# Two bias rows of a vision tower: from TensorE and ScalarE to adds on GpSimd

## The reference, cut to what matters

```
def _L0_ffn_ref(x, W1, b1, W2, b2):              # mix
    h = jax.nn.gelu(tril_apply(x, W1, b1), approximate=False)
    return tril_apply(h, W2, b2)                 # h @ tril(W2).T + b2
...
# dif: o is the attention's result, normalized over groups of 32 features of one image
xn = (xc - mu) * rsqrt(var + EPS)
xn = xn * gn_w[None, :, None] + gn_b[None, :, None]
y = xn.transpose(0, 2, 1) @ out_w.T + out_b
...
h = h + _L0_ffn_ref(_layernorm(h), ...)
h = h + _L1_attn_ref(_layernorm(h), ...)
```

## Time and profile before

| | us |
|---|---|
| median of three executions | 389.16 |
| the three executions | 389.21, 387.92, 389.16 |
| the profiled execution's own time | 389.98 |
| its span in the profile | 388.3 |
| TensorE busy | 347.7 (90%) |
| VectorE busy | 233.7 (60%) |
| ScalarE busy | 220.9 (57%) |
| GpSimd busy | 197.4 (51%) |

### The profile page before, as it was taken

The page is one execution under the profiler, slowest core; times in us unless marked ns, Lnnn a source line. Parts: engine busy times, 40 slices in busy tenths (PEclk is TensorE's granted clock), DMA queues, the critical chain, the costliest instruction groups (busy, mean ns, idle before and its releaser), DMA issues.

```text
span 388.3 us, 11371 instructions
## 1 busy us (share of the span) xinstructions
PE 347.7 (90%) x4424; PEld 315.2 (81%) x4424; DVE 233.7 (60%) x615; ACT 220.9 (57%) x640; POOL 197.4 (51%) x312
## 2 busy tenths in 40 slices
PE   8969799999988999997899899499999999999950
PEld 8748687887866889696778788399999999999950
DVE  1446788763489899897868985623335433333314
ACT  1247677777659876677488563103555555555520
POOL 3169687587841112236345767720555555555550
PEclk9999999999999999998999999559999999999995
DMA  7999924000000000000000100037899989999206
GB/s 277 374 391 334 150 28 125 2 2 1 2 3 0 3 3 2 3 2 3 3 3 2 33 9 13 15 95 202 272 320 316 322 308 316 327 324 314 85 9 182
DMA packets 21239, 50.20 MB, mean 129 GB/s; under 512 B 4116, under 2 KB 10340, under 8 KB 21058
## 3 DMA queue, kind: packets, MB, share of 16 engines
q1 hardware_dynamic: 18146, 46.96, 37.9%
q0 software_dynamic: 3040, 2.52, 2.4%
HBM read 43.97 MB, written 7.72 MB: 133 GB/s over the span
## 4 chain that ended last, share of the span: by engine, by line
PE 57%; DVE 12%; ACT 11%; POOL 9%; DMA 6%; issue 4%; SPq 1%; POOLq 0%; DVEq 0%
PE bank L728 34%; PE scores L728 18%; DMA lambdas<-in_lambdas 4%; ACT work L1037 4%; PE bank L803 3%; ACT norm L1037 3%; POOL rstd L613 3%; DVE mx L1266 2%; DVE stats L1203 2%; DVE work L1275 1%; ACT src L1037 1%; PE bank L979 1%; POOL rstd L611 1%; ACT xrow L1037 1%; POOL norm L664 1%
## 5 line engine op out<-in xcount | busy, mean ns | idle before, releaser
L1037 ACT ACTIVATE work<-scores,b1T 128x72 f32<-128x72 f32 x256 | 61.3, 322 | 66.9 <-PE scores L728 66.9
L728 PE MATMUL bank<-ring,work 128*72 128x128 f32 x512 | 97.3, 274 | 0.0
L720 POOL DMA_INDIRECT expert_rows<-work,put_u x64 | 59.9, 935 | 61.7 <-issue 37.7
L728 PE MATMUL scores<-work,ring 128*128 128x72 f32 x512 | 89.0, 258 | 0.2 <-ACT work L1037 0.2
L728 PEld LDWEIGHTS scores<-work,ring 128*128 128x128 f32 x512 | 76.9, 191 | 0.3 <-issue 0.3
L728 PE MATMUL bank<-wT 128*128 128x128 f32 x504 | 72.3, 283 | 2.7 <-ACT work L1037 2.7
L728 PEld LDWEIGHTS bank<-wT 128*128 128x128 f32 x504 | 63.8, 193 | 5.7 <-ACT work L1037 3.1
L1037 ACT ACTIVATE work<-bank 128x288 f32<-128x288 f32 (+3 forms) x136 | 46.7, 376 | 34.4 <-PE bank L728 27.0
L1437 DVE TENSOR_SCALAR work<-bank,work 72x128 f32<-72x128 f32 x64 | 22.2, 347 | 67.5 <-PE bank L728 67.5
L728 PEld LDWEIGHTS bank<-ring,work 128*72 128x72 f32 x512 | 53.8, 145 | 0.2 <-ACT work L1037 0.2
L611 POOL TENSOR_SCALAR rstd<-mv 96x3 f32<-96x3 f32 x32 | 10.1, 315 | 54.8 <-DVE mv L1206 53.6
(11 more groups left out here) (159 smaller groups left out, 594.2 us busy)
## 6 DMA issues: line engine op xcount, KB each, us to landing
ring<-in_experts SPq DMA_DIRECT2D x64, 512.0 KB, 5.0
work<-in_patches SPq DMA_DIRECT2D x3, 864.0 KB, 10.6
slot_rows<-hid SPq DMA_DIRECT2D x1, 2340.0 KB, 30.2
work<-slot_rows SPq DMA_DIRECT2D x7, 292.5 KB
wT<-in_weights SPq DMA_DIRECT2D x1, 1664.0 KB, 13.9
expert_rows<-mid POOLq DMA_DIRECT2D x2, 576.0 KB, 5.1
ring<-expert_rows SPq DMA_DIRECT2D x4, 288.0 KB, 4.0
expert_rows<-work,put_u POOLq DMA_INDIRECT x64, 4.4
```

The source lines that it names most:

```text
L720: pool.indirect_dma_start(out=ytok[:, :], out_offset=bass.IndirectOffsetOnAxis(ap=put_u[:, e:e + 1], axis=0), in_=ys[0:CAP, e % NY, :], in ...
L728: return nc.tensor.matmul(o, a, b, start=start, stop=stop)
L1037: return nc.scalar.activation(o, i, f, **kw)
```

## The change

Neither bias goes through TensorE any more. GpSimd gets a stage mix_norm_b (mid = h + L0_ffn_b2) behind each mix_norm_a and a stage dif_norm_b (mid = h + L1_attn_out_b) behind each dif_norm_a, four of each, and VectorE's mix_out and dif_out add the product to mid instead of to h. The bias of the group normalization is folded into the row L1_attn_out_b once, early: one matmul on TensorE (stage fold:0 behind rope_qk:0), one add on VectorE (fold:0 behind rope_qk:0). The eight opening matmuls and ScalarE's four gn_apply go away. The idle matmuls stay as they were.

```
 ORDERS_FOUND = {     # two places of the pe order, one of act, one of dve, three of pool
-    tok_shift:3 rope_qk:0 tok_turn:3 rope_v:0 rope_scores:0 src_turn:1 ...
+    tok_shift:3 rope_qk:0 fold:0 tok_turn:3 rope_v:0 rope_scores:0 src_turn:1 ...
...
-    x1_norm_a:3 x2_norm_a:1 x2_norm_b:1 x1_affine:3 mix_norm_a:1 dif_norm_a:0 x2_norm_a:2 x2_norm_a:3 x2_norm_b:2
+    x1_norm_a:3 x2_norm_a:1 x2_norm_b:1 x1_affine:3 mix_norm_a:1 mix_norm_b:1 dif_norm_a:0 dif_norm_b:0 x2_norm_a:2 x2_norm_a:3 x2_norm_b:2
...
+                if stage == "mix_norm_b":
+
+                    pool.tensor_tensor(tiles(mid, b), tiles(h, b), row("L0_ffn_b2"), ALU.add).then_inc(S["mix_based"], 1)
+                if stage == "dif_norm_b":
+
+                    pool.wait_ge(S["folded"], 1)
+                    pool.tensor_tensor(tiles(mid, b), tiles(h, b), row("L1_attn_out_b"), ALU.add).then_inc(S["dif_based"], 1)
...
-            def biased(job, name):
-
-                o = fill(pe, job)
-                pe.wait_ge(S["rows_in"], 16)
-                mm(o[0:TP, 0:TPB * D], const("ones")[0:1, :], rows[0:1, ROWS.index(name), :].unsqueeze(1).broadcast_to([1, TPB, D]),
-                   start=True, stop=False)
...
                 elif stage == "mix_out":
-                    biased((stage, b, 0), "L0_ffn_b2")
                     pe.wait_ge(S["hid_ready"], hid_count["mix_in", b])
-                    tokens((stage, b, 0), lambda k, i: hid[:, 0, b % 2, TP * i:TP * i + TP], [block_of("L0_ffn_W2")], open_=True)
+                    tokens((stage, b, 0), lambda k, i: hid[:, 0, b % 2, TP * i:TP * i + TP], [block_of("L0_ffn_W2")])
...
                 elif stage == "dif_out":
-                    biased((stage, b, 0), "L1_attn_out_b")
-                    pe.wait_ge(S["square_ready"], square_n["gn_apply", b])
-                    tokens((stage, b, 0), ctx_tile, [block_of("L1_attn_out_w")], open_=True)
+                    pe.wait_ge(S["gn_scaled"], b + 1)
+                    tokens((stage, b, 0), ctx_tile, [block_of("L1_attn_out_w")])
+                elif stage == "fold":
+
+                    pe.wait_ge(S["cols_in"], 16)
+                    pe.wait_ge(S["weights_in"], 16)
+                    o = fill(pe, (stage, b, 0))
+                    mm(o[0:TP, 0:D], col("L1_attn_gn_b").broadcast_to([D, TP]), block_of("L1_attn_out_w")).then_inc(filled((stage, b, 0)), 1)
...
-                elif stage == "gn_apply":
-
-                    act.wait_ge(S["gn_scaled"], b + 1)
-                    go(ctxT[:, tok], ctxT[:, tok], ACT.Identity, bias=col("L1_attn_gn_b")).then_inc(S["square_ready"], 1)
...
-                    base = {"rope": src, "net": mid, "mix": h, "dif": h, "moe": src}[name]
+                    base = {"rope": src, "net": mid, "mix": mid, "dif": mid, "moe": src}[name]
+                    if stage in ("mix_out", "dif_out"):
+                        dve.wait_ge(S["mix_based" if stage == "mix_out" else "dif_based"], b + 1)
...
+                elif stage == "fold":
+                    dve.wait_ge(S["rows_in"], 16)
+                    o = read(dve, (stage, b, 0))
+                    r = rows[:, ROWS.index("L1_attn_out_b"), :]
+                    v.tensor_tensor(r, r, o[0:TP, 0:D], ALU.add).then_inc(S["folded"], 1)
```

31 lines of the change are left out of this document (15 added, 16 removed).

## The result

The changed kernel took 392.75 us (median of 7 executions, 391.55 to 393.91); before, run beside it, took 389.16 us (7 executions, 387.15 to 390.31). The ratio is 1.0092, 95% interval 1.0064 to 1.0121: slower by 3.6 us. The prediction was 389.0 with a range to 391.8; the result lies above it.

What follows compares the result with a forecast made beforehand. The prediction saw a relay between engines, no single full one, and the expert loop unchanged. Losses of 2.3 and 0.3 less gains of 0.6, 0.95, 0.8 and 0.4 gave -0.15 us: 389.0 us, range 386.8 to 391.8.

Steps and rivals of the forecast that it cites:

- Eight adds, 2.3 us: GpSimd's new adds, 1.0 us each: 0.3 and 2.0 us on the chain, five hidden in waits, together 2.3 us lost.
- L1327 less than 2 us late: Sign of a wrong prediction: VectorE's add of x2_norm_b:3 delayed under 2 us, meaning GpSimd's chain had slack.
- fold, 0.3: The added matmul in TensorE's unbroken early piece of 7.33 us: 0.3 us lost, between nothing and 0.90.
- mix_out:3, -0.6, and the other opening matmuls of mix, nothing: Near 130 us, mix_out:3's product starts earlier, gaining 0.6 us; mix_out:0 to :2 gain nothing, the chain being elsewhere.
- dif_out:0, -0.95: Near 161 us, removing the opening matmul and gn_apply:0 ends VectorE's wait for the product: 0.95 us gained.
- dif_out:2, -0.8: Removing its opening matmul moves up everything behind it, ahead of the scores at 190.38: 0.8 us gained.
- gn_apply:3, -0.4: ScalarE's instruction at 198.42, on the chain between the exponential and moe_turn:2, goes away: 0.4 us gained.
- Rival "the clock": The adds open a hole in TensorE's work and its clock falls again: about 1 us, 390.0, at most 390.7; chance 0.15.
- a fall between 104 and 125: Sign of a wrong prediction: TensorE's granted clock falls between 104 and 125 us.
- Rival "the holes don't close": The losses stay and the four gains fail, VectorE holding the chain: 391.8 with all gone, 390.6 with two; chance 0.15.
- Rival "faster": The relay re-forms earlier, with the delay halved and one more 0.81 us earned: 386.9; chance 0.14.
- Rival "contention": GpSimd's adds slow VectorE's two-input SBUF instructions, up to 0.78 us each: 389.8 with one meeting, 391.3 with three; chance 0.06.

Runs made afterwards that it cites:

- e1: The changed kernel with 13 instead of 10 idle (warming) matmuls at the start of TensorE's program: ratio 1.0006 to before.
- e11: The kernel before with only dif's half of the change, its first two adds in GpSimd's waits, and 11 warming matmuls: ratio 0.9928 to before.
- e5: The changed kernel run again, unedited: ratio 1.0031 to before.
- e10: The changed kernel with 13 instead of 10 warming matmuls, the same kernel as e1: ratio 1.0024 to before.
- e13: The changed kernel run once more, unedited: ratio 1.0101 to before.
- e18: The changed kernel with 13 instead of 10 warming matmuls, the same kernel as e1 and e10: ratio 1.0002 to before.
- e17: The kernel e15 with 13 instead of 10 warming matmuls: ratio 1.0039 to before.
- e15: The kernel before with mix's half of the change but without its four adds, mix's bias left out of the output: ratio 1.0096 to before.
- e6: The changed kernel with dif_norm_b:0 and dif_norm_b:1 moved behind mix_norm_b:3 on GpSimd: ratio 0.9986 to before.
- e7: The kernel before with only dif's half of the change, its first two adds in GpSimd's waits, and 8 warming matmuls: ratio 0.9934 to before.
- e8: As e7, with mix_out:3's opening matmul also replaced by an add, and 9 warming matmuls: ratio 0.9966 to before.
- e12: As e8, with 12 instead of 9 warming matmuls: ratio 0.9959 to before.
- e14: The kernel before with only mix's half of the change, its four adds included: ratio 1.0103 to before.

## Why the prediction was wrong

The step that failed is a term that the sum, "2.3 + 0.3 - 0.6 - 0.95 - 0.8 - 0.4 = -0.15 us", does not have: it takes TensorE, where no instruction of it is changed, to run on as before. It did not in dif_scores2:2. VectorE's shifts, read from -0.99, show where the sum went off:

- up to mix_out:3 the change lost 2.41 us; forecast were 2.3 - 0.6 = 1.7. The other 0.7 is the fall of the clock near 107 (0.8 by the shift right behind it, see below), which the prediction had as a rival outside the sum.
- from mix_out:3 to dif_out:1 it lost 1.63 us; forecast was a gain of 0.95. These 2.6 us come with the stop of TensorE and the fall of the clock at its end; e1, the same edit without them, gained 0.78 there.
- from dif_out:1 to 204 us it gained 1.09 us; forecast were 0.8 + 0.4 = 1.2.

By the prediction's own steps:

- *Eight adds, 2.3 us.* Right: 2.23 us, 0.31 and 1.92, and 0.99 to 1.00 us each. The five in waits cost nothing that can be seen. Its sign of "L1327 less than 2 us late" did not come if the head start is taken off: 1.23 us as the profiles stand, 2.2 from -0.99. The Trainium skill's rule (GPSIMD Engine Reference, section 4.1) that speaks against GpSimd for such work bears on size, not on the outcome: 0.99 to 1.00 us on GpSimd against 0.55 for VectorE's add, yet dif's half has four such adds and is 0.7% faster: all four stand in waits.
- *fold, 0.3.* Its two passes took 0.42 us together, at 32.51 in the changed kernel; VectorE's shift was -0.54 ahead of it (23 to 32 us) and -0.56 behind it (38 to 45 us), so it cost nothing.
- *mix_out:3, -0.6, and the other opening matmuls of mix, nothing.* The first is right in the profile: VectorE's wait went from 0.91 to 0.30. The second overlooked that the one of mix_out:1 filled a wait for hid: without it TensorE stands idle for 0.93 us there, part of the hole in which the clock fell.
- *dif_out:0, -0.95.* Nearly right without the stop: no wait left in e11, and 0.78 us gained by dif_out:1 in ten kernels. In the changed kernel a wait of 0.39 stayed, since the stop and the second fall of the clock had put back TensorE's work ahead of it.
- *dif_out:2, -0.8, and gn_apply:3, -0.4.* Right: from dif_out:1 to moe_scores:1 the shift went from +3.05 to +2.08, and to moe_turn:2 it went down 0.40 more.
- *Rival "the clock", about 1 us, 0.15.* The mechanism came as described, near 107, in every kernel that has both adds in GpSimd's piece and four idle matmuls (after, e1, e5, e10, e13, e18), and in none with the hole filled or one add less. It cost some 0.8 us of the relay (VectorE's shift goes from +1.23 at 105.92 to +2.02 at 111.09, before's times). The prediction had named a fall between 104 and 125 as a sign that it is wrong, and the sign came. Too small was its reach: a clock that falls is not one event. The Trainium skill (TensorE: Matmul & The Clock Gate, section "HAM oscillation — how this bites in real kernels") tells of a kernel that goes back to the lower clock in wait after wait; the runs agree in kind, with four falls in the changed kernel's profile ahead of its last stretch, at 107.12, 151.50, 185.63 and 247.07, the first three behind waits or a stop of 0.94 to 1.90 us.
- *Missing altogether: the stop.* It is the largest piece. In the changed kernel VectorE lost 1.63 us up to the maxima of dif_scores2:2, and the 0.95 forecast behind them did not show.
- *Rival "the holes don't close", 391.8.* It did not happen: three of the four gains came in whole, and of dif_out:0's wait 0.57 of 0.96 us went. That its time is nearest to the result is chance.
- *Rival "faster".* Its 386.9 takes the -0.15 off twice; 389.16 - 0.15 - 1.15 - 0.81 is 387.05. Nothing hangs on it.
- *Rival "contention".* No sign of it: VectorE was busy for 233.7 us before and 234.0 after, with one instruction more.

What the stop is, the trace tells in part. The page has a row "q8 instruction: 36, 0.59, 0.6%" in both kernels: 36 transfers of 16 KB. The DMA view of 134 to 155 us, in 40 slices of 0.525 us, first before, then after, then e18 (each 31 is one such transfer):

```profile
GB/s 0 0 0 0 0 0 31 0 0 0 0 0 0 0 0 0 0 0 0 0 0 0 31 0 0 0 0 0 0 31 0 0 0 0 0 0 0 0 0 0
```
```profile
GB/s 0 0 0 0 0 0 0 31 0 0 0 0 0 0 0 0 0 0 0 0 0 0 0 0 0 0 0 0 31 0 0 0 0 0 0 0 31 0 0 0
```
```profile
GB/s 0 0 0 0 0 0 0 0 31 0 0 0 0 0 0 0 0 0 0 0 0 0 0 31 0 0 0 0 0 0 0 0 31 0 0 0 0 0 0 0
```

By the records of the transfers the second comes 8.4 us after the first in before and 7.7 in e18, but 10.9 us after it in the changed kernel, at 148.97, while the scores run; the stop begins at 149.45. TensorE has 9225 instructions in the trace (loads, matmuls and waits), 256 to each transfer, so I read them as pieces of its program. In all eight kernels with the stop it lies right behind the same count, 3777 instructions, whichever these are, and the transfer ahead of it started when TensorE was at 3724 to 3740; in the other eleven and in before it started at 3506 to 3534 (before has 0.13 us at 3777, the others nothing). The transfer ahead of it is the fourteenth of the 36. Another stop, of 0.6 to 1.8 us near 45 us, lies behind instruction 705 in all twenty, 12 x 256 earlier, and the transfer ahead of that one is the second, 12 earlier.

The times of the transfers tie the two together. The late transfer takes 0.96 to 1.38 us, and in all eight kernels TensorE goes on 1.25 to 1.39 us after it has ended: a longer transfer makes a longer stop (0.96 and 1.75 us in the changed kernel, 1.38 and 2.23 in e17). In the twelve others TensorE comes to instruction 3777 only 1.41 us (before, with its 0.13 us) to 2.54 us after the transfer's end. At 705 it goes on 1.47 to 1.77 us after the end. So at neither place did TensorE start a new piece within 1.2 us of the end of the transfer ahead of it. That the late piece of program makes the stop is shown by these times in twenty profiles, not by an experiment on the piece itself. What makes the piece late stays open: three warming matmuls removed it in the changed kernel (three of three) but not in e15, e6 removed it with TensorE's program untouched, and of e7 and e8, which have dif_scores2:2 at the same place of the program (its first instruction is 3672), only e8 has it. Open too is how the whole time follows: e5 lost only 0.31% and e17 0.39% with the stop in the profile, and e8 and e12 cannot be told apart; and so is whether the falls near 185 that last twice as long (e14, e15) are a consequence of the stop.

## What to carry to other kernels

A sum of terms over a relay is only as good as the stretches it calls unchanged: look in the trace of before for idle time of TensorE that nothing releases, and give such a stop a rival of its own, since an edit of the program or of its waits can move it. Not each such idle time is one: the 0.77 and 0.69 us of the earlier trace rows lie at instructions 3942 and 4962, a multiple of 256 behind neither 705 nor 3777. And ask of an instruction that you take out what it filled: a matmul that ran inside a wait leaves a hole. A kernel that lies within 1% of another should be compared in more than one layout (a few idle matmuls more or less at the start) before the edit gets the blame or the praise; here dif's half held its 0.7% in two layouts, while the whole change went from 1.0092, 1.0031 and 1.0101 to 1.0006, 1.0024 and 1.0002 by three matmuls that compute nothing. And split a change in halves early: one half of this one, with its adds in waits, was a gain.
